# A four-layer block kernel on one core: scores in pairs of 64 rows, a slot table of its own for every beat, and FP32 products in four column groups

## What is computed

```
def attention(x):                # 16 heads of 16, one key and one value head shared by all
    q = (x @ w_q.T).reshape(B, S, 16, 16); k = x @ w_k.T; v = x @ w_v.T
    a = softmax(einsum('bshd,btd->bhst', q, k) * softmax_scale)
    return einsum('bhst,btd->bshd', a, v).reshape(B, S, 256) @ w_out.T
def ffn(x):                      # 256 -> 1024 -> 256, W1 and W2 rounded to -1, 0, 1
    return gelu(x @ ternary(W1).T + b1) @ ternary(W2).T + b2
def recurrent(x):                # a decaying sum along the positions, then a gated recurrence
    xn = layernorm(x) * norm_g + norm_b
    states = A_pow * cumsum((xn @ B_w.T + B_b) / max(A_pow, 1e-8)); u = states @ C_w.T + C_b
    for t in positions:          # cat = [u_t, h]
        f1, f2 = tanh(cat @ ff1_w.T + ff1_b), tanh(cat @ ff2_w.T + ff2_b)
        g = sigmoid((cat @ ta_w.T + ta_b) * 0.1 + cat @ tb_w.T + tb_b)
        h = f1 * (1 - g) + g * f2
    return x + h_all @ out_w.T + out_b
def quantised(x): return fp6(x) @ fp6(weight).T + bias       # blocks of 32, one scale each
x = ln(x + attention(x)); x = ln(x + ffn(x)); x = ln(x + recurrent(x)); x = ln(x + quantised(x))
```

## Time and profile before

| | before |
|---|---|
| median of 3 runs | 1874.36 us (1873.85 to 1876.61) |
| profiled execution, span | 1875.9 us |
| TensorE matmul busy | 1757.2 us, 94% |
| VectorE | 1413.3 us, 75% |
| ScalarE | 1173.6 us, 63% |
| GpSimd | 1020.8 us, 54% |
| mean granted TensorE clock | 0.967 |
| HBM read, written | 31.50 MB, 18.35 MB |

### The profile page before, as it was taken

One profiled execution on the slowest core, in us unless ns is written; L12 is line 12 of the kernel. 1 busy time (PEld: TensorE's weight loads), 2 busy tenths in 40 slices (PEclk: granted clock), 3 DMA queues, 4 the chain that ended last, 5 costly groups with the idle time before them and its releaser, 6 DMA issues.

```text
span 1875.9 us, 74519 instructions
## 1 busy us (share of the span) xinstructions
PE 1757.2 (94%) x29935; PEld 1283.4 (68%) x29935; DVE 1413.3 (75%) x2997; ACT 1173.6 (63%) x2795; POOL 1020.8 (54%) x3192
## 2 busy tenths in 40 slices
PE   6879899999999999999999999999999999999875
PEld 4545567777777777777777777777777777777653
DVE  4656767787778877787778877787778777787454
ACT  3445666666666666666666666666666666666521
POOL 2102245666566666666566666666566656666632
PEclk8889999999999999999999999999999999999965
DMA  8511111111111111111111111111111111111000
GB/s 228 162 30 37 38 45 40 42 47 48 45 43 43 51 45 45 39 50 45 45 43 46 50 45 42 42 51 45 45 41 48 48 45 45 41 48 29 20 22 21
DMA packets 140912, 92.94 MB, mean 50 GB/s; under 512 B 20196, under 2 KB 139800, under 8 KB 140568
## 3 DMA queue, kind: packets, MB, share of 16 engines
q1 hardware_dynamic: 136368, 87.91, 17.2%
q10 hardware_dynamic: 4200, 0.27, 0.2%
HBM read 31.50 MB, written 18.35 MB: 27 GB/s over the span
## 4 chain that ended last, share of the span: by engine, by line
PE 57%; DVE 19%; SPq 7%; issue 6%; DMA 4%; POOL 3%; ACT 3%; DVEq 0%; ACTq 0%; POOLq 0%
PE gen_bank L766 10%; PE gen_bank L868 9%; PE value_bank L729 8%; DVE nmax L1121 8%; PE score_bank L697 7%; PE max_banks L559 6%; SPq L414 5%; DMA lowstage<-qpiece 3%; PE gate_bank L761 2%; DVE stats L1242 2%; DVE qaug L1137 2%; PE gen_bank L581 2%; PE gen_bank L807 2%; PE gen_bank L776 2%; SPq L417 2%
## 5 line engine op out<-in xcount | busy, mean ns | idle before, releaser
L1068 ACT ACTIVATE probs<-score_bank 128x512 f32<-128x512 f32 x1024 | 604.2, 600 | 238.8 <-PE score_bank L697 226.0
L1121 DVE TENSOR_REDUCE nmax<-max_banks 128x2 f32<-128x1024 f32 x512 | 622.6, 1216 | 89.5 <-PE max_banks L561 85.5
L697 PE MATMUL score_bank<-qaug,kaug 98*128 98x512 bf16 x1024 | 370.9, 387 | 2.4 <-ACT probs L1068 1.4
L729 PE MATMUL value_bank<-probs,vaug 128*32 128x128 f32 x8192 | 332.6, 280 | 0.0
L729 PEld LDWEIGHTS value_bank<-probs,vaug 128*32 128x32 f32 x8192 | 193.9, 109 | 123.2 <-issue 93.6
L1656 POOL TENSOR_TENSOR diff<-gates 128x16 f32<-128x16 f32 x472 | 126.3, 267 | 235.1 <-ACT gates L1074 233.8
L766 PE MATMUL gen_bank<-w2T,hT 128*128 128x256 f32 x1024 | 252.1, 389 | 0.0
L559 PE MATMUL max_banks<-kaug,qaug 64*128 64x512 bf16 x512 | 199.9, 390 | 37.4 <-DVE nmax L1121 35.1
L766 PEld LDWEIGHTS gen_bank<-w2T,hT 128*128 128x128 f32 x1024 | 184.3, 190 | 33.7 <-issue 13.8
L561 PE MATMUL max_banks<-kaug,qlow 64*128 64x512 bf16 x512 | 200.8, 392 | 0.0
L868 PE MATMUL gen_bank<-x1piece,w1Tb 128*128 128x128 bf16 x3072 | 195.2, 220 | 0.5 <-DVE x1rest L1396 0.5
(11 more groups left out here) (233 smaller groups left out, 2968.2 us busy)
## 6 DMA issues: line engine op xcount, KB each, us to landing
qstage<-qpiece SPq DMA_DIRECT2D x384, 64.0 KB
lowstage<-qpiece SPq DMA_DIRECT2D x192, 64.0 KB
xt<-in_L_attn_x SPq DMA_DIRECT2D x64, 128.0 KB
xk<-in_L_attn_x SPq DMA_DIRECT2D x16, 512.0 KB, 7.4
residual<-x2s SPq DMA_DIRECT2D x64, 128.0 KB
x2f<-residual SPq DMA_DIRECT2D x64, 128.0 KB
out<-x SPq DMA_DIRECT2D x64, 128.0 KB
raw<-in_L_ffn_W SPq DMA_DIRECT2D x2, 1024.0 KB, 8.3
```

Of the source, the lines that this page charges most:

```text
L697: pe.matmul(score_bank[t % 2][:, :], kaug[0:AUG, r, tt, u, :], qaug[:, r, u, :, :].rearrange("p h s -> p (h s)"), start=True, stop=True).t ...
L729: last = pe.matmul(value_bank[32 * g:32 * g + 32, :].rearrange("p (k t) -> p k t", k=HG)[:, :, uv * BLOCK_POS:(uv + 1) * BLOCK_POS], vaug[ ...
L1068: act.activation(probs[:, t % 4, :], score_bank[t % 2][:, :], ACT.Exp).then_inc(exp_done, 1)
L1121: dve.tensor_reduce(nmax[:, m % 2, at:at + 3:2], max_banks[:, :, :], AX_X, ALU.max, negate=True).then_inc(max_taken, 1)
```

## The change

The kernel does the same mathematics with these differences.

- Queries and keys are split in two F32R pieces (high, low) in place of three BF16 ones. Four products of 16 rows fill 62 rows (the low-low product leaves out its last two features), two more hold the maximum: a contraction of 64. The layout is made twice, in rows 0 to 63 and 64 to 127, and a beat multiplies two key blocks at once into two score banks. One exponential reads both banks (1024 columns). There are 8 beats for 16 ticks.
- The maxima use the same layout, 62 rows in each half. qlow and lowstage are gone. The query moves are 8 DMAs, the maxima's 4.
- The second layer multiplies two F32R halves of hT (hhi by ScalarE, hlo half by VectorE and half by GpSimd) with F32R weights.
- Q, INPUT, PROJ, B, OUT and LAST are issued in four column groups of 32.
- LN1, LN2 and LN4 are finished by ScalarE (Identity with scale and shift; GpSimd makes the shift). States move from VectorE to GpSimd. The block scales take two steps less.
- A tile time has 256 slots. Every beat of scores, pair, values, step, exponential, tanh, maximum and mix has a slot of its own (BEAT_AT), and SyncE has a table.
- Setup: keys are stored and placed as FP32 halves, and part of SBUF is shared between setup and later tensors.

```diff
-TICKS = 16
-SLOTS = 4 * TICKS
+BEATS = 8
+SLOTS = 32 * BEATS
...
+PE_AT = dict(INPUT=0, F2_0=275, F2_1=280, F2_2=285, F2_3=285, F2_4=286, F2_5=288, F2_6=299, F2_7=302, TURND=279, LAST=322, XT=50, Q=12, OUT=128, OT=65, ATT=73, PROJ=90, TURNX=149, B=160, X1T=217, NM=204, FFN1A=247, FFN1B=249)
+ACT_AT = dict(OT=44, TURND=339, XT=104, Q=29, Q8=253, TURNX=196, ATT=145, X1T=230, GELUA=238, GELUB=239, X1=194, X2=178, X4=496)
+DVE_AT = dict(Q=23, X4R=362, X2R=52, OT=62, X3R=171, X3=239, QUANT=240, XN=148, LN1=157, BS=190, SCAN=236, ORDER=182, X1P=216, HLOA=240, NM=216)
+POOL_AT = dict(LN4=418, LN3=97, LN2=6, LNI=8, QIN=192, X2S=77, XD=214, X3B=193, LN1=15, X1B=116, STATES=165, HLOB=219)
+SP_AT = dict(MOVE=15, X2F=200, STORE=89, OUTST=406, XLD=59, NMPLACE=95)
+BEAT_AT = dict(
+    SCORES=(19, 61, 89, 107, 137, 157, 178, 231),
+    PAIR=(18, 55, 87, 102, 140, 202, 236, 250),
+    VALUES=(11, 68, 100, 128, 151, 157, 224, 252),
+    STEP=(15, 51, 72, 93, 135, 156, 166, 229),
+    EXP=(86, 121, 165, 181, 186, 227, 228, 236),
+    TANH=(46, 90, 125, 170, 181, 196, 227, 235),
+    MAX=(17, 26, 60, 107, 160, 190, 213, 233),
+    MIX=(3, 4, 12, 13, 20, 34, 96, 157),
+)
...
-                for g, piece in enumerate((0, 0, 0, 1, 1, 2)):
-                    sp.dma_start(by_head(qstage[g * DK:(g + 1) * DK, :, :]),
-                                 qpiece[:, piece, :, :].rearrange("p k t -> p (k t)")).then_inc(q_placed, 16)
+                for at, g, piece in MOVES:
+                    dims = min(DK, SPLIT - g * DK)
+                    sp.dma_start(qstage[at + g * DK:at + g * DK + dims, :, :].bitcast(F32).rearrange("d (h k) t -> d h (k t)", k=KT),
+                                 qhalf[0:dims * H // KT, piece, :, :].bitcast(F32).rearrange("p k t -> p (k t)")).then_inc(q_placed, 16)
...
+            def in_quarters(out, weights, moving, start, stop):
+
+                for q in range(0, P, 32):
+                    last = pe.matmul(out(q), weights[:, q:q + 32], moving, start=start, stop=stop, tile_position=(0, q), skip_group_check=True)
+                return last
...
+            def scores(n, r, beat):
+
+                u, at = divmod(beat, 2)
+                if beat == 0:
+                    pe.wait_ge(nm_placed, 64 * (n + 1))
+                wait(pe, exp_done, BEATS * n + beat)
+                pe.matmul(score_bank[0][:, :], kaug[0:HALF, r, 2 * at, u, :], qaug[0:HALF, n % QR, u, :, :].rearrange("p h s -> p (h s)"),
+                          start=True, stop=True, tile_position=(0, 0))
+                pe.matmul(score_bank[1][:, :], kaug[HALF:P, r, 2 * at + 1, u, :], qaug[HALF:P, n % QR, u, :, :].rearrange("p h s -> p (h s)"),
+                          start=True, stop=True, tile_position=(HALF, 0)).then_inc(scores_ready, 2)
...
-                return pe.matmul(gen_bank[0][:, 0:D], hT[:, f, :], w2T[:, f, :], start=(f == 0), stop=(f == FT - 1), skip_group_check=True)
+                pe.matmul(gen_bank[0][:, 0:D], hhi[:, f, :], w2T[:, f, :], start=(f == 0), stop=False, skip_group_check=True)
+                return pe.matmul(gen_bank[0][:, 0:D], hlo[:, f, :], w2T[:, f, :], start=False, stop=(f == FT - 1), skip_group_check=True)
...
+                            act.wait_ge(emptied[half], use(half, name, m) + 1)
+                            rows_of = slice(4 * half, 4 * half + 4)
+                            act.activation(hhi[:, rows_of, :], hT[:, rows_of, :], ACT.Copy).then_inc(h_hi, 1)
...
+                        act.wait_ge(scores_ready, 2 * (z + 1))
+                        wait(act, pv_done, z - 1)
+                        act.activation(probs[:, beat % 2, :, :], score_banks[:, :, :], ACT.Exp).then_inc(exp_done, 1)
...
-                dve.tensor_copy(qlow[HALF:P, m % 2, :, :, :].rearrange("p u h s -> p h u s"),
-                                lowstage[HALF:P, H // 2:H, :].rearrange("p h (u s) -> p h u s", u=GROUP)).then_inc(q_ordered, 1)
-                dve.tensor_copy(qaug[0:SPLIT, m % R, :, :, :].rearrange("p u h s -> p h u s"),
+                dve.tensor_copy(qaug[:, m % QR, :, :, :].rearrange("p u h s -> p h u s"),
                                 qstage[:, :, :].rearrange("p h (u s) -> p h u s", u=GROUP)).then_inc(q_ordered, 1)
...
+            def low_half(m):
+
+                dve.wait_ge(h_hi, 2 * m + 1)
+                dve.tensor_tensor(hlo[:, 0:FT // 2, :], hT[:, 0:FT // 2, :], hhi[:, 0:FT // 2, :], ALU.subtract).then_inc(h_lo[0], 1)
...
+            def make_states(m):
+
+                cm, rm = divmod(m, R)
+                pool.wait_ge(ssm_step, 2 * m + 2)
+                pool.tensor_tensor(states[:, cm % 2:cm % 2 + 1, :, rm * GROUP:(rm + 1) * GROUP].rearrange("p a s g -> p g (a s)"), csum[:, rm, :, :],
+                                   apow[:, cm * BLOCK_POS:(cm + 1) * BLOCK_POS].unsqueeze(1).to_broadcast([P, GROUP, BLOCK_POS]),
+                                   ALU.mult).then_inc(states_made, 1)
```

More of the change, by code:

```diff
@@ L713, in next_pair @@
-            def next_pair(n, t):
-                u, tt = divmod(t, 4)
+                for at in range(SLOTS):
+                    beat = beat_at("SCORES", at)
+                    if beat is not None and live(n):
+                        scores(n, r, beat)
+                    beat = beat_at("PAIR", at)
+                    if beat is not None:
+                        next_pair(*divmod(BEATS * n + beat + 1, BEATS))
+                    beat = beat_at("VALUES", at)
+                    if beat is not None:
+                        if beat:
+                            values(n, r, beat - 1)
+                        else:
+                            values(n - 1, (r - 1) % R, BEATS - 1)
+                    beat = beat_at("STEP", at)
+                    if beat is not None and live(n + LEAD["REC"]):
+                        step(n + LEAD["REC"], beat, gate_bank)
+                    general(n, at)
@@ new lines, in general @@
+                m = mine("TURND", "OUT")
+                if m is not None:
+                    pe.wait_ge(emptied[1], use(1, "TURND", m))
+                    pe.wait_ge(xd_ready, m + 1)
+                    turn_tile(g1, xd).then_inc(filled[1], 1)
+                m = mine("LAST", "OUT")
+                if m is not None:
+                    pe.wait_ge(emptied[1], use(1, "LAST", m))
+                    pe.wait_ge(emptied[1], use(1, "TURND", m) + 1)
+                    for k in range(KT):
+                        last = in_quarters(lambda q: g1[q:q + 32, 0:D], xdT[:, k, :], wdT[:, k, :], k == 0, k == KT - 1)
+                    last.then_inc(filled[1], 1)
@@ new lines, in general @@
+                m = mine("OT", "FFN")
+                if m is not None:
+                    wait(pe, emptied[0], use(0, "OT", m))
+                    pe.wait_ge(values_out, m + 1)
+                    for k in range(HG):
+                        last = pe.transpose(g0[:, k * P:(k + 1) * P], oT[:, k, :], ident[:, :])
+                    last.then_inc(filled[0], 1)
+                m = mine("ATT", "FFN")
+                if m is not None:
+                    pe.wait_ge(emptied[0], use(0, "ATT", m))
+                    turn_tile(g0, att).then_inc(filled[0], 1)
@@ L1235, in _ @@
                     order_queries((b - 7) // 8)
-            for pair in range(B + MORE - FIRST_MAX, TICKS // 2):
+            for pair in range(B + MORE - FIRST_MAX, BEATS):
                 take_maxima(0, pair)
@@ L1651, in tile_time @@
+                for at in range(SLOTS):
+                    k = beat_at("MIX", at)
                     m = n + LEAD["REC"]
-                    if live(m) and t % 2:
-                        k = t // 2
+                    if k is not None and live(m):
                         j = STEPS * m + k
```

965 lines of the change are left out of this document (467 added, 498 removed).

## The result

The changed kernel takes 1770.09 us (median, 1766.09 to 1771.92) beside 1875.28 us for the kernel before on the same chip: a ratio of 0.9437, 95% interval 0.9423 to 0.9452. 105 us are gone where 195 were forecast; the time lies inside the range of the prediction (1615 to 1800) and outside the forecast's own (1640 to 1730).

A forecast was written before the change was run, and what follows sets the result against it. TensorE's own queue was taken as the bound: 21.7 us of instructions, 1.2 of gaps and 0.3 more waits make a 23.2 us tile, saving 3.1 x 63 = 195 us; with setup +1, 1682 profiled, 1680 median. Range 1615 to 1800, forecast's own 1640 to 1730.

The forecast's parts named there:

- TensorE is the bound, its queue read from start to start: TensorE's instructions per tile, timed from one start to the next: 25.1 of 26.3 us before, 21.7 after.
- F32R at one pass: Scores, pairs and second layer: F32R streams like BF16, 0.22 us a pair, 0.11 a second-layer record of 256 columns.
- 23 changes at the price of BF16 rows: TensorE's changes of tile shape per tile: 23 against 24 before, 0.10 us each, 2.3 us.
- Column groups: +0.2 for the groups, one change of shape less: TensorE's FP32 products in four groups of 32 columns: 4.35 us becomes 4.54, changes of shape 24 become 23.
- The order copy at 1.23 us: VectorE's copy of 2048 query elements, now 4-byte: 1.23 us at two elements a cycle, 2.29 at one; 0.69 in BF16.
- The maxima's way just fits: Maxima's path from NM to the next SCORES: 8.0 us within TensorE's 8.4; 1 us of period if VectorE is later.
- Setup +1, tail 0: Outside the tiles: setup 1 us longer from key moves with more bytes and larger GpSimd memsets; tail's steps as before.
- The coupled queues: Rival: VectorE's slow copy, GpSimd's 5.1 us or the maxima's way holds the tile: 24 to 25.7, 1730 to 1840 us; 0.21.
- GpSimd's 5.1 us: GpSimd work queued between a tile's last recurrent step and the next tile's first: about 5.1 us, just fitting TensorE's 6.5.
- Two or more passes: Rival: F32R matmuls need more passes; two give 2014 us, four near 2680, slower than before; chance 0.10.
- the serial pair: Rival: F32R row pairs don't run side by side, +3.5 us on TensorE, 1855 to 1885 us; chance 0.05.
- the better slots: Rival: the new slots cut waits to 0.5 us a tile, period 22.2, 1615 us; chance 0.08.

The follow-up runs named there:

- e2: Changed kernel without the eight second-layer products with the low half of the hidden values (part of the result missing): 1779.48 us, ratio 0.9497.
- e8: Changed kernel with ScalarE's copy of the turned xd after its first exponential and tanh, and TensorE's turning of the next x later: 1772.20 us, ratio 0.9456.
- the sequences alone: Separate kernel repeating only short matmul sequences, none of the kernel's work: pair and four column groups took 0.68 us in BF16, 0.78 in F32R.
- e5: Changed kernel with GpSimd's addition of the second layer's bias to x1 moved 42 places later, away from VectorE's cast: 1772.49 us, ratio 0.9454.
- e4: Changed kernel with the setup placing the last group of key pieces after the moves of the third query group: 1768.25 us, ratio 0.9442.
- e3: Changed kernel with GpSimd's second low-half subtraction cut from 512 columns to 16 (part of the result missing): 1771.26 us, ratio 0.9446.
- e9: Changed kernel with e8's two moves and without the eight low-half second-layer products (part of the result missing): 1765.47 us, ratio 0.9419.

## Why the prediction came out as it did

- *TensorE is the bound, its queue read from start to start.* Half right. Written as 21.7 us of instructions and 1.5 of gaps and waits, the tile of 24.3 has some 23.2 of instructions and 1.1 of waits (0.30 for hlo, 0.29 for x1piece, 0.33 and 0.14 for hseq). But 0.96 us of these instructions can go without the tile getting shorter (e2), so the sum wasn't what held it. The lowest tile with TensorE nearly always on the chain is e8's, 23.93.
- *F32R at one pass.* Right for the streaming (records 0.11 to 0.12 apart, pairs 0.226). The step that failed is the term beside it, 23 changes at the price of BF16 rows. In the tile from 899.71 to 924.01, pairs and scores take 5.68 us; the terms gave 1.76 + 1.76 + nine changes of 0.10 = 4.42. The 1.26 us are nine visits of 0.14 on the mean, near the 0.10 (one pair) and 0.12 (two pairs, 1.02 for 0.68 + 0.22) of the sequences alone. The second layer without the 0.30 of its wait took 2.34 with the turning of xd, 0.36 over the terms. The prediction itself says that no F32R matmul is in the trace, and it bounded the passes; the weight load was bounded by nothing.
- *First layer.* 48 records took 3.07 us for 2.69: 0.29 is the wait for VectorE's cast beside GpSimd (e5), 0.09 is left open.
- *Column groups: +0.2 for the groups, one change of shape less.* The first is 0. The second hid what the groups do: 23 holds only with them. Undone, they cost 1.0 to 1.2 us on the loop directly and 0.75 to 0.9 through GpSimd.
- *VectorE.* The order copy at 1.23 us: measured 1227 ns. HLOA at 0.69: 640 ns. What was not priced is what a 4-byte copy does to others. An operation of GpSimd that takes 0.22 alone took up to 1.28 beside it. The Trainium skill, "SBUF — State Buffer", "SBUF: two separate sides", says that the two engines share a port pair which one of them holds for a whole instruction; the trace agrees, 1.25 and 1.28 us beside a copy of 1.23, 0.48 beside copies of 0.44 and, in the kernel before, 0.77 beside one of 0.69.
- *ScalarE 19.5 us a tile.* Busy 879.90 in 1100 us, or 45.2 tiles: 19.5. *GpSimd 18.0:* 778.14 / 45.2 = 17.2.
- *The maxima's way just fits.* Right in most tiles: ahead of the scores, TensorE's loader waited 4.3 us for it in 45 tiles. The chain of waits runs over that transfer in 10 of the 45, of 24.26 to 25.39 us.
- *Setup +1, tail 0.* Wrong: +15 and +4. The setup's DMA engines were busy for 95% of the first 100 us at 213 GB/s (68% at 188 before), and SyncE's queue placed key group 3 ahead of queries that TensorE needed first (6 us, e4). "More bytes: +1 us" was no working.
- *The rivals.* The coupled queues named 24 to 25.7 us and 1730 to 1840 us, and this is what came, 24.33 and 1770. The range of the forecast held by this rival, and for other reasons than it gave: its three places were not the ones. The copy wasn't slow, GpSimd's 5.1 us (e3) didn't hold, and the maxima's way only in some tiles. The loop over the turning of xd, the table load and the inner normalisation was not in it, and neither was what F32R costs at a change. Two or more passes, the serial pair and the better slots are excluded by rows.

In sum: 24.33 - 23.2 = 1.13 us x 63 = 71 us in the tiles and 19 - 1 = 18 in setup and tail make 89; from 1682 to 1769.6 it is 88, since the prediction rounded 3.12 us to 3.1. What stays open: which single thing sets 24.2. TensorE's queue (at most 23.9), the loop (24.2) and VectorE's and GpSimd's way to the first step (e9) lie within a few tenths, and every edit that relieved one met the next. Open too is what lengthens the half of the tiles that take more than 24.28.

## What to carry to other kernels

Price an instruction kind that the trace doesn't show by its weight load and by its neighbours too, not only by its passes. When the busiest engine is at 98%, follow the chain of waits round one whole period before taking its sum for the period: here 0.96 us of work that was removed beside ScalarE's table load bought nothing (e2). In a kernel whose order is a table, each edit shifts all engines against each other, so look at the spread of single periods (23.93 and 24.97) and not at their mean alone. And look in the trace of before at whether short operations grow beside a long copy on another engine.
